# Routed experts of a gated cross-attention block: expert rows split ahead of their transposes, five down products, pairwise sums of a token's rows, and another order of the last router pass

## The reference

```python
x2 = rmsnorm(hid, ln2_w).reshape(-1, h)
logits = x2 @ gate_w.T
probs = jax.nn.softmax(logits, axis=-1)
top_w, top_i = jax.lax.top_k(probs, TOPK)              # TOPK = 4 of E = 16
top_w = top_w / jnp.sum(top_w, axis=-1, keepdims=True)
wfull = jnp.sum(jax.nn.one_hot(top_i, E, dtype=x2.dtype) * top_w[..., None], axis=1)
gu = jnp.einsum('th,eih->tei', x2, w1)
g, u = (gu[..., :I], gu[..., I:])                      # I = 176
act = jax.nn.silu(g) * u
down = jnp.einsum('tei,ehi->teh', act, w2)
routed = jnp.einsum('te,teh->th', wfull, down)
sgu = x2 @ sh_gu_w.T
shared = jax.nn.silu(sg) * su @ sh_down_w.T
return hid + (routed + shared).reshape(b, s, h)
```

## Time and profile before

| what | value |
|---|---|
| median of 3 runs | 1019.81 us (1018.04 to 1022.72) |
| the profiled execution, its own time | 1017.26 us |
| its span | 1015.4 us |
| mean granted clock of TensorE | 0.927 of full speed |
| busy over the span | PE 876.7 us (86%), DVE 796.8 (78%), ACT 638.3 (63%), POOL 525.6 (52%) |
| DMA | 84.08 MB, mean 83 GB/s |

### The profile page before, as it was taken

The page is one execution under the profiler, slowest core; times in us unless marked ns, Lnnn a source line. Parts: engine busy times, 40 slices in busy tenths (PEclk is TensorE's granted clock), DMA queues, the critical chain, the costliest instruction groups (busy, mean ns, idle before and its releaser), DMA issues. The chain is left out here.

```text
span 1015.4 us, 23692 instructions
## 1 busy us (share of the span) xinstructions
PE 876.7 (86%) x8201; PEld 626.9 (62%) x8201; DVE 796.8 (78%) x1867; ACT 638.3 (63%) x1571; POOL 525.6 (52%) x616
## 2 busy tenths in 40 slices
PE   3466689999999899999998999989996699999850
PEld 1243356777777676676676777767763478777730
DVE  4689878788888988988988776787667677777666
ACT  3678868887888876888877766757631044444410
POOL 5688864546546463877662553203445244444542
PEclk9577569999999999999999999999999799999985
DMA  5222510101000011211001114031324444444273
GB/s 179 91 77 73 165 34 22 30 22 50 17 22 25 22 43 37 78 42 63 17 22 30 60 70 146 22 116 56 112 78 152 123 139 138 145 136 139 80 294 146
DMA packets 47827, 84.08 MB, mean 83 GB/s; under 512 B 6448, under 2 KB 36528, under 8 KB 47664
## 3 DMA queue, kind: packets, MB, share of 16 engines
q1 hardware_dynamic: 39792, 61.60, 19.7%
q0 software_dynamic: 6912, 19.93, 5.4%
q10 hardware_dynamic: 1008, 1.03, 0.3%
HBM read 52.92 MB, written 31.98 MB: 84 GB/s over the span
## 5 line engine op out<-in xcount | busy, mean ns | idle before, releaser
L663 PE MATMUL ps<-whi,ar 128*128 128x256 f16 (+1 forms) x880 | 248.2, 282 | 16.7 <-DVE ar L1764 9.9
L664 PE MATMUL ps<-wlo,ar 128*128 128x256 f16 (+1 forms) x880 | 247.8, 282 | 0.0
L665 PE MATMUL ps<-whi,ar 128*128 128x256 f16 (+1 forms) x880 | 247.8, 282 | 0.0
L1541 POOL TENSOR_TENSOR ar<-ar,sm 128x512 f32<-128x512 f32 x64 | 69.8, 1090 | 155.7 <-DVE sm L1830 155.6
L1450 POOL TENSOR_TENSOR sm<-sm,mhalf 128x1 f32<-128x1 f32 (+2 forms) x72 | 126.5, 1756 | 6.0
L1592 POOL DMA_INDIRECT y<-ar,idx x80 | 76.7, 959 | 100.3 <-ACT ar L1421 87.0
L663 PE MATMUL ps<-ar 128*128 128x128 f16 (+1 forms) x768 | 117.2, 206 | 8.4 <-DVE ar L1714 4.1
L664 PE MATMUL ps<-ar 128*128 128x128 f16 (+1 forms) x768 | 117.1, 206 | 0.0
L665 PE MATMUL ps<-ar 128*128 128x128 f16 (+1 forms) x768 | 117.0, 206 | 0.0
L663 PEld LDWEIGHTS ps<-whi,ar 128*128 128x128 f16 x880 | 86.7, 99 | 41.9 <-DVE ar L1764 10.7
L663 PE MATMUL ps<-ar,whi 128*128 128x512 f16 x292 | 112.1, 384 | 0.1
(11 more groups left out here) (231 smaller groups left out, 2231.9 us busy)
## 6 DMA issues: line engine op xcount, KB each, us to landing
ar<-xg SPq DMA_DIRECT2D x80, 144.0 KB, 2.2
ar<-in_wall SPq DMA_DIRECT2D x16, 512.0 KB, 3.7
stg<-in_wall SPq DMA_DIRECT2D x32, 188.0 KB, 2.4
ar<-in_wall SPq DMA_DIRECT2D x8, 608.0 KB, 4.6
whi<-y SPq DMA_DIRECT2D x4, 1024.0 KB, 8.1
wlo<-y SPq DMA_DIRECT2D x4, 1024.0 KB, 17.3
xg<-in_pad SPq DMA_DIRECT2D x1, 2304.0 KB, 10.6
xg<-x1d SPq DMA_DIRECT2D x4, 512.0 KB, 4.4
```

Source lines behind the costliest of these rows:

```text
L663: mm(o, l_hi, r_hi, start=start, stop=False, skip_group_check=True)
L664: mm(o, l_hi, r_lo, start=False, stop=False, skip_group_check=True)
L665: return mm(o, l_lo, r_hi, start=False, stop=stop, skip_group_check=True)
L1541: TT(pr, pr, eq4.unsqueeze(2).broadcast_to([P, GB, S]), ALU.mult).then_inc(sem("p_n"), 1)
```

## The change

1. **Split first.** The activated rows of a pair are split into f16 parts before they are transposed. ACT writes the high part of all 176 features (`cut_tile(u)`, right behind `tanh(u)`). DVE writes the low part of the first 128 features to a block of its own, and the low part of the other 48 into rows 64 to 111 of the block whose rows 0 to 47 hold their high part (`lo_tile(u)`, two operations). PE transposes three f16 blocks for each tile instead of two f32 ones, and ACT copies the six turned blocks in one operation (`copy_tile`).
2. **Five products.** The down weights of the 48 features stand twice in their 128 rows, at 0 and at 64. One matmul with the high weights and one with the low weights then cover high and low part; with three for the first 128 features that is five for a tile instead of six. (The product of low by low is now taken along for the 48.)
3. **Row sums.** `mix` adds the first two rows of a token to the other two in place, then the two sums; both are DVE's, and `add_z` moves from POOL to DVE, behind each `mix`.
4. **Router first.** In the last group DVE does `r_lo` before `s_mid(1, 0)`, both `r_copy` before `s_add(0)`, and `r_soft` before `s_mid(1, 2)`; PE does `r_logits` before `s_down(1, 0)`.
5. **Bookkeeping.** The semaphore `sel_free` goes: SP's load of pair u waits until the index of pair u - 4 has been made. DVE zeroes two small tiles before the first pair, and a matmul that cleared a bank is gone.

```diff
 EREST = EI - P
+HALF = P // 2
 GU = 2 * EI
...
         m_p = [words(512 * b, 2 * EI).rearrange("p (i n) -> p i n", i=2) for b in range(2)]
-        m_hl = [halves(1024 + 512 * b, 512).rearrange("p (l c t) -> p l c t", l=2, c=2) for b in range(2)]
+        m_s = [halves(RT + 384 * b, 384).rearrange("p (i n) -> p i n", i=2) for b in range(2)]
+        m_T = [halves(1024 + 512 * b, 384).rearrange("p (c t) -> p c t", c=3) for b in range(2)]
         idn32 = cs[:, C_IDN:C_IDN + P]
...
                     sp.wait_ge(sem("tx_free"), u + 1)
-                    sp.wait_ge(sem("sel_free"), u + 1)
+                    sp.wait_ge(sem("idx"), u - 3)
                 both = sp.value_load(rowtab[0:1, u:u + 1], min_val=0, max_val=512 * 512 - 1)
...
             s_gate_up(1, 1)
+            r_logits(g, NG * NH)
             s_down(1, 0)
-            r_logits(g, NG * NH)
             s_gate_up(1, 2)
...
             def turn_m(u, b):
-                pe.wait_ge(sem("me_v"), u + (CH + 4))
-                pe.wait_ge(sem("me_lo"), u + (CH + 2))
-                o = bank(MB).rearrange("p (c i t) -> p c i t", c=2, i=2)
+                pe.wait_ge(sem("me_lo"), u + (CH + 3))
+                pe.wait_ge(sem("mT_cut"), u)
+                o = bank16(MB)[:, 0:6 * P].rearrange("p (c i t) -> p c i t", c=3, i=2)
                 for i in range(2):
-                    nc.tensor.transpose(o[:, 0, i, :], m_p[b][:, i, 0:P], idn32)
-                    last = nc.tensor.transpose(o[0:EREST, 1, i, :], m_p[b][:, i, P:EI], idn32)
+                    for n in range(3):
+                        last = nc.tensor.transpose(o[:, n, i, :], m_s[b][:, i, n * P:(n + 1) * P], idn)
                 last.then_inc(sem("mt_ps"), 1)
             def down_tile(u, b, off):
-                pe.wait_ge(sem("me_lo"), u + (CH + 3))
+                pe.wait_ge(sem("mT_cut"), u + 1)
                 pe.wait_ge(sem("d_bank"), u + 1)
                 for i in range(2):
-                    tt = slice(i * P, (i + 1) * P)
-                    for n in range(2):
-                        c = off[i] + (KC * GU + n * D)
-                        last = three(bank(DB[b])[:, i * D:(i + 1) * D], m_hl[b][:, 0, n, tt], m_hl[b][:, 1, n, tt],
-                                     wcol(whi, c, D), wcol(wlo, c, D), n == 0, n == 1)
+                    o = bank(DB[b])[:, i * D:(i + 1) * D]
+                    m_hi, m_rest, m_lo = (m_T[b][:, n, i * P:(i + 1) * P] for n in range(3))
+                    c, c_rest = (off[i] + (KC * GU + n * D) for n in range(2))
+                    three(o, m_hi, m_lo, wcol(whi, c, D), wcol(wlo, c, D), True, False)
+                    mm(o, m_rest, wcol(whi, c_rest, D), start=False, stop=False, skip_group_check=True)
+                    last = mm(o, m_rest, wcol(wlo, c_rest, D), start=False, stop=True, skip_group_check=True)
                 last.then_inc(sem("d_ps"), 1)
-            mm(bank(MB), idn, zero.broadcast_to([P, 512]), start=True, stop=True, skip_group_check=True)
             pe.wait_ge(sem("stage_cut"), NH + SMALL + 1 + LATE)
...
             def cut_tile(u, b):
+                act.wait_ge(sem("me_v"), u + (CH + 4))
+                act.wait_ge(sem("mt_ps"), max(0, u - 1))
+                A(m_s[b][:, :, 0:EI], m_p[b], ACT.Copy).then_inc(sem("me_hi"), 1)
+
+            def copy_tile(u, b):
+
                 act.wait_ge(sem("mt_ps"), u + 1)
                 act.wait_ge(sem("d_ps"), u + (CH + 2))
-                A(m_hl[b][:, 0].rearrange("p c t -> p (c t)"), bank(MB), ACT.Copy).then_inc(sem("me_hi"), 1)
+                A(m_T[b].rearrange("p c t -> p (c t)"), bank16(MB)[:, 0:6 * P], ACT.Copy).then_inc(sem("mT_cut"), 1)
             def store(u, v):
...
                     tanh(u, u % 2)
+                    cut_tile(u, u % 2)
                 if 1 <= u <= PAIRS:
-                    cut_tile(u - 1, (u - 1) % 2)
+                    copy_tile(u - 1, (u - 1) % 2)
                 if u >= 2:
...
                     sem("me_lo"), 1)
-
-            def add_z(m):
-
-                pool.wait_ge(sem("y_sum"), m + 1)
-                pool.wait_ge(sem("fin"), m // 2 + 1)
-                TT(ob[m], ob[m], zfin[m // 2][:, m % 2 * 512:m % 2 * 512 + 512], ALU.add).then_inc(sem("mixed"), 1)
             def put(g, n):
...
             s_lo(SHL, 2)
-            for m in range(NB // 2):
-                add_z(m)
         @block.vector
...
             r_xr(g)
+            r_lo(g)
             s_mid(1, 0)
-            r_lo(g)
-            s_add(0)
             r_copy(g, 0, SB_)
             r_copy(g, 1, TB)
+            s_add(0)
             s_mid(1, 1)
             r_logits(g)
+            r_soft(g)
             s_mid(1, 2)
-            r_soft(g)
             r_ranks(g)
...
             dve.sem_inc(sem("me_v"), 2)
-            dve.sem_inc(sem("sel_free"), 4)
             def take(u, b):
...
                                xinw[v][:, i, D:D + 2 * NE].rearrange("p (w e) -> p w e", w=2), ALU.is_equal, ALU.mult)
-                last.then_inc(sem("sel_free"), 1)
-                dve.wait_ge(sem("sel_free"), u + 5)
+                last.then_inc(sem("dve_step"), 1)
+                dve.wait_ge(sem("dve_step"), 2 * u + (NG * RC + TC + 1))
                 V.tensor_reduce(selw[b][:, 64:68], selw[b][:, 0:64].rearrange("p (i e) -> p i e", i=4),
...
                 got = selw[v % 2][:, 64:68].rearrange("p (i w) -> p i w", w=2)
-                dve.wait_ge(sem("dve_step"), u + (NG * RC + TC + 1))
+                dve.wait_ge(sem("dve_step"), 2 * u + (NG * RC + TC + 2))
                 dve.wait_ge(sem("y_free"), u + 1)
...
                 dve.wait_ge(sem("me_hi"), u + (CH + 1))
-                TT(m_hl[b][:, 1].rearrange("p c t -> p (c t)"), bank(MB),
-                   m_hl[b][:, 0].rearrange("p c t -> p (c t)"), ALU.subtract).then_inc(sem("me_lo"), 1)
-
+                TT(m_s[b][:, :, 2 * P:3 * P], m_p[b][:, :, 0:P], m_s[b][:, :, 0:P], ALU.subtract)
+                TT(m_s[b][:, :, P + HALF:P + HALF + EREST], m_p[b][:, :, P:EI], m_s[b][:, :, P:EI],
+                   ALU.subtract).then_inc(sem("me_lo"), 1)
+
+            for b in range(2):
+                V.memset(m_s[b][:, :, EI:2 * P], 0.0)
             for u in range(2):
...
                 select(u, u, 32)
-            for u in range(PAIRS + 1):
-                if u < PAIRS:
-                    expert(u, u % 2)
-                    index(u, u % 4)
+            for u in range(PAIRS):
+                expert(u, u % 2)
+                index(u, u % 4)
                 if u + 2 < PAIRS:
...
                     select(u + 2, (u + 2) % 4, 32 * ((u + 2) // 4 + 1))
-                if u >= 1:
-                    lo_tile(u - 1, (u - 1) % 2)
+                lo_tile(u, u % 2)
             def mix(m):
-                dve.wait_ge(sem(f"yb{yb_sem(m)}"), yb_full(m))
-                V.tensor_reduce(ob[m].rearrange("p (a d) -> p a d", a=2),
-                                yb[m].rearrange("p (a k d) -> p a d k", a=2, k=TOPK), AX.X, ALU.add).then_inc(sem("y_sum"), 1)
+                rows = yb[m].rearrange("p (a c) -> p a c", a=2)
+                dve.wait_ge(sem(f"yb{m}"), 16)
+                TT(rows[:, :, 0:2 * D], rows[:, :, 0:2 * D], rows[:, :, 2 * D:4 * D], ALU.add).then_inc(sem("y_sum"), 1)
+                dve.wait_ge(sem("y_sum"), 2 * m + 1)
+                TT(ob[m].rearrange("p (a d) -> p a d", a=2), rows[:, :, 0:D], rows[:, :, D:2 * D], ALU.add).then_inc(
+                    sem("y_sum"), 1)
+
+            def add_z(m):
+
+                dve.wait_ge(sem("y_sum"), 2 * m + 2)
+                dve.wait_ge(sem("fin"), m // 2 + 1)
+                TT(ob[m], ob[m], zfin[m // 2][:, m % 2 * 512:m % 2 * 512 + 512], ALU.add).then_inc(sem("mixed"), 1)
             s_mid(SHL, 0)
...
             s_mid(SHL, 2)
-            mix(0)
-            mix(1)
-            s_add(SHL)
-            for m in range(2, NB // 2):
+            for m in range(NB // 2):
                 mix(m)
+                if m == 1:
+                    s_add(SHL)
+                add_z(m)
 def kernel(x, ctx_1024, g_xattn, g_ffn, L0_xattn_Wq, L0_xattn_bq, L0_xattn_Wk, L0_xattn_bk,
...
     dn[:, :EI] = w2.transpose(0, 2, 1)
+    dn[:, P + P // 2:P + P // 2 + EREST] = dn[:, P:EI]
     dn = dn.reshape(NE, 2, P, D).transpose(2, 0, 1, 3).reshape(P, NE, 2 * D)
...
```

## The result

| | before | after |
|---|---|---|
| median | 1018.9 us (1017.6 to 1022.7) | 992.4 us (991.2 to 995.1) |
| ratio of after to before | | 0.9737, 95% interval 0.9703 to 0.9772 |
| profiled execution: time, span | 1017.3, 1015.4 | 991.2, 989.3 |
| up to the experts' first transposes | 798.5 | 794.8 |
| from there to the first gather's issue | 173.3 | 164.0 |

(Before has one run more here than ahead of the prediction.) The change makes the kernel 26.5 us faster; the forecast was 23.9, and 992.4 lies in the range. The two spans differ by 26.2 us: 3.7 before the experts, 9.3 in them, 8.9 from the gathers to the last output, and 4.3 behind that output, where the forecast had nothing.

The account below looks back on a forecast made before the run. The prediction took TensorE to bound the expert pairs, DVE's router chain the scatters before them, and DVE's row sums the tail. Terms -12.5 - 2.4 - 9.0 = -23.9 us against the 1019.8 median gave 996 us, range 988 to 1005.

Parts of the forecast that it names:

- Part 1: Expert pairs on TensorE: -12.5 us in all, between -6 and -14.
- period of a pair: Expert stage: a pair on TensorE goes from 3.98 to 3.66 us, giving -12.8 us over 40 pairs.
- -0.22 and -0.10: Expert pair on TensorE: -0.22 us from two fewer down products, -0.10 from six f16 transposes replacing four f32 ones.
- ACT's loop: Expert pair on ACT, from tanh to next tanh: 3.44 us, under TensorE's 3.66 by 0.22.
- rival 1: Expert pair: ACT's loop becomes the bound; period 3.79 and time 1001, or 1009 at period 3.98; chance 14%.
- The middle between 0.60 and 1.02 for the copy: Expert pair on ACT: the copy of 768 f16 elements was taken at 0.81 us.
- the sum of -12.5: Expert stage: -12.8 for 40 pairs, +1.0 for index waits, -0.7 at the stage's end.
- The step that loads rows now waits for a later count of the index and loads four pairs ahead: nothing: Expert stage, SP's row loads: the changed wait was costed at nothing.
- The charge of +1.0 for the index waits: Expert stage: row-index waits for POOL's late scatters grow with shorter pairs, +1.0 us, between 0 and 1.6.
- Part 2: Router before the experts: first scatter leaves 2.4 us earlier, between 0 and -3.9; all sixteen scatters move with it.
- Part 3: Tail after the experts: three DVE operations replace each row sum and POOL's add, -9.0 us, between -6 and -10.

Follow-up runs that it names:

- the sixth product: A sixth down product for each expert tile (low activations by low weights), added to the early load: 999.7 us, 7.0 above the early load beside it.
- the experts' part alone: Kernel before with only points 1 and 2 (split first, five products), rows loaded as early as before: 1008.2 us, ratio 0.9882.
- the early load: The change, but SP loads a pair's rows after the select of pair u - 4, not its index: 993.4 us, ratio 0.9739; repeats 994.3 and 992.6.
- the router alone: Kernel before with only the router's new order on DVE and PE: 1019.1 us, ratio 0.9979.
- the tail alone: Kernel before with only the tail's new sums, pairwise adds and last add all on DVE: 1008.4 us, ratio 0.9879.
- the one add alone: The early load with only the last of the eight shared adds back on POOL: 995.9 us, 1.7 above the early load beside it.

## Why the prediction was right, and where it was not

**What bounds the kernel** was right. TensorE paces the pair (the sixth product), and the tail was DVE's.

**Part 1, period of a pair: right.** 3.66, with -0.22 and -0.10 as worked out. But 40 times 0.32 was too much: 35 periods run at TensorE's pace, 11.2 us and not 12.8; the first four are set by the first rows' way through the engines.

**Part 1, ACT's loop: right.** 3.41 against 3.44 by the estimate; rival 1 would have begun to bind with 0.25 us more. The middle between 0.60 and 1.02 for the copy was within 0.02 of 0.79.

**Part 1, the sum of -12.5: wrong for the change's profile, -9.3.** The step that failed is "The step that loads rows now waits for a later count of the index and loads four pairs ahead: nothing". I had counted pairs and not the time between the index and the transposes: 1.5 us to SP's second issue, then 4.0 until TensorE needs the rows. A landing took 2.2 us in the median, and 3.5 or 4.2 a few times, and then TensorE stands. With the wait undone the stretch is 161.0, 161.3 and 162.0, a gain of 11.3 to 12.3; in the experts' part alone 12.9. So the wait makes 2.2 of the 3.2 (163.6 against 161.4), and the later third pair another 0.8. In the medians the wait's price isn't seen. The charge of +1.0 for the index waits came out as a fall by 2.2 in the change, and about as in before or up to 1.7 above it with the early load. The 3.3 of before was itself one execution's: the router's and the tail's part alone, with the old pairs, have 1.3 and 0.8.

**Part 2, -2.4: right.** The first scatter leaves 1.9 earlier in the profile, and the router alone gives 2.1 by the ratio of its times. That the experts start 3.7 earlier has two more causes: the sixteen scatters took 19.4 us instead of 20.8 from first to last, and this execution was 0.6 ahead when the router's stage began. The shorter scatters go with the new order: they took 20.8 to 21.0 us in the three kernels with the old one, and 19.4 to 20.5 in the eleven with the new one. Each of the three has a scatter of 2.1 us, where most take 0.96; seven of the eleven have none over 1.3. The forecast let the sixteen move as a block. Why they shorten no run shows.

**Part 3, -9.0: right.** 8.9, and 8.2 in the tail alone. DVE's pace and the data's come out alike: the last gather lands at 983.35, and DVE ends 3.3 us behind it. The Trainium skill (VectorE: DVE Perf Modes, the section on the perf-mode tier table) puts `tensor_reduce` at the same 1x rate as an f32 `tensor_tensor`, which it gives 2.29 us for 2048 elements. By that rate this part would have been a loss of 2; the tail alone won 8.2. The trace disagrees with it for this strided view, as its row of 3.62 had said.

**What the sum left out: -4.3 behind the last output.** Part 3 ended the old kernel with POOL's add at 1008.6 and took the rest, 1008.6 to 1015.4, as a constant. It was not: 4.3 of it was the program's end waiting for POOL. The trace of before had shown this in SP's last wait. The two errors, +3.2 and -4.3, nearly cancel, which is luck; with the 1.3 more before the experts the forecast was too small by 2.3 against the spans and 2.6 against the medians.

## What to carry to other kernels

Where an edit swaps the event that a transfer waits for, lay the path out in us: from the new event over the issue to the slowest landing shown, against the moment when the consumer comes; counts of pairs ahead say nothing. At the end of a program look at what follows the last output: an engine with late work can hold the end, so small last operations belong on an engine that closes fast. A busy share of two thirds is no room: ACT's loop had 0.25 us of a pair's 3.66.

## What the runs showed of the hardware that I had not expected

- **POOL closes slowly.** From the start of its last add its closing drain's record is 7.93 us long, in the kernel before and with the one add alone; DVE's, with its last add, is 0.73. Where POOL works last, 4.7 us pass between the last landing and the end, otherwise 0.4.
- **DVE and POOL slow each other.** At 965.18 DVE's add of two SBUF sources took 1.52 us instead of 0.69, while POOL's operation at 964.38 took 1.78 instead of 1.15. The Trainium skill (SBUF — State Buffer, "Who interferes with whom") says that a DVE operation with two SBUF inputs contends with a POOL operation that reads SBUF; both rows agree. It happened once in the tail and cost at most 0.8 us.
- **A long stand costs twice.** After 2.98 us without rows TensorE's granted clock was 0.52, and the next 3.5 us of work ran at it; after 1.56 us it did not fall.
